# Two layers of attention and feed-forward on one core: VectorE's order inside a head of the index stage, with the selection's best-eights put between the two sums

## The reference, cut to what matters

```python
iq = (hidden_states @ idx_wq_w).reshape(b, s, IDX_H, IDX_D)          # IDX_H = 16, IDX_D = 128
ik = hidden_states @ idx_wk_w
iw = hidden_states @ idx_weights_w * IDX_H ** (-0.5)
idx_scores = jnp.einsum('bqn,bnqk->bqk', iw, jax.nn.relu(jnp.einsum('bqnd,bkd->bnqk', iq, ik))) * IDX_D ** (-0.5)
idx_scores = jnp.where(causal, idx_scores, -jnp.inf)
_, topk_idx = jax.lax.top_k(idx_scores, TOPK)                        # TOPK = 128
mask = topk_mask & causal
scores = jnp.where(mask[:, None], scores, -jnp.inf)                  # the 32 attention heads use it
```

## Time and profile before

| | us |
|---|---|
| median of three runs | 1416.42 |
| lowest and highest of them | 1415.38, 1418.27 |
| the profiled execution's own time | 1415.27 |
| its span, first to last instruction | 1413.5 |

### The profile page before, as it was taken

How to read it: one execution, slowest core, us unless ns; L and a number is a source line. 1 busy time by engine, 2 the same in 40 slices (tenths; PEclk the granted TensorE clock), 3 DMA queues, 4 the chain that set the end, 5 groups by cost and what they waited for, 6 DMA issues and landing times.

```text
span 1413.5 us, 21378 instructions
## 1 busy us (share of the span) xinstructions
PE 1308.7 (93%) x7147; PEld 1095.1 (77%) x7147; DVE 1089.0 (77%) x2246; ACT 822.2 (58%) x1816; POOL 715.1 (51%) x705
## 2 busy tenths in 40 slices
PE   4868999999899999998689999999999999999998
PEld 3756888888789887876367888888888888888876
DVE  6676334343647798999979889889899989989976
ACT  3653432222246766764567776766677676667761
POOL 3660300010037789984845665565565565566524
PEclk9978999999999999998589999999999999999999
DMA  5640300000212436646620000000000000000021
GB/s 201 208 157 27 118 13 1 1 21 0 70 39 68 125 84 198 209 141 230 207 63 14 24 6 29 29 29 29 29 13 17 29 29 29 29 29 1 16 83 60
DMA packets 83707, 95.53 MB, mean 68 GB/s; under 512 B 11792, under 2 KB 59280, under 8 KB 83088
## 3 DMA queue, kind: packets, MB, share of 16 engines
q1 hardware_dynamic: 83600, 94.17, 20.9%
HBM read 75.27 MB, written 18.87 MB: 67 GB/s over the span
## 4 chain that ended last, share of the span: by engine, by line
PE 73%; DVE 15%; ACT 3%; issue 3%; DMA 2%; POOL 1%; SPq 1%; DVEq 1%; ACTq 0%
PE ps L361 18%; PE ps L362 17%; PE ps L363 17%; PE ps L1986 9%; PE ps L2006 3%; PE ps L2005 3%; DVE rop L1523 1%; DVE xn_l L1573 1%; DVE pm L1553 1%; DVE rop L1521 1%; DVE acc L1498 1%; PE ps L1885 1%; DVE rop L1522 1%; PE ps L1684 1%; DVE top L1511 1%
## 5 line engine op out<-in xcount | busy, mean ns | idle before, releaser
L785 POOL TENSOR_SCALAR pm<-pm,smx 128x128 f32<-128x128 f32 (+1 forms) x255 | 189.3, 751 | 206.5 <-DVE smx L1560 206.4
L1114 ACT ACTIVATE pm<-pm,smx 128x128 f32<-128x128 f32 (+7 forms) x256 | 197.2, 772 | 36.6 <-DVE smx L1553 34.9
L1553 DVE CUSTOM_DVE_ANT_0 pm<-ps,mbias 128x128 f32<-128x128 f32 (+7 forms) x256 | 191.3, 752 | 27.2 <-PE ps L363 12.4
L1986 PE MATMUL ps<-ident,pm 128*128 128x128 f32 x1152 | 174.1, 276 | 7.7 <-DVE xn_l L1573 2.1
L1120 ACT ACTIVATE xn_h<-ps 128x512 fp32r<-128x512 f32 (+3 forms) x256 | 128.7, 513 | 82.1 <-PE ps L1986 79.1
L1573 DVE TENSOR_TENSOR xn_l<-ps,xn_h 128x512 fp32r<-128x512 f32 (+3 forms) x256 | 144.3, 587 | 24.3 <-ACT xn_h L1120 23.2
L1986 PEld LDWEIGHTS ps<-ident,pm 128*128 128x128 f32 x1152 | 134.0, 141 | 33.7 <-issue 11.8
L361 PE MATMUL ps<-latT_l,qc_h 128*128 128x512 f32 (+4 forms) x384 | 142.9, 372 | 16.9 <-DVE smx L1553 8.7
L363 PE MATMUL ps<-latT_h,qc_h 128*128 128x512 f32 (+4 forms) x384 | 132.4, 345 | 0.0
L362 PE MATMUL ps<-latT_h,qc_l 128*128 128x512 f32 (+4 forms) x384 | 132.2, 344 | 0.0
L361 PEld LDWEIGHTS ps<-latT_l,qc_h 128*128 128x128 f32 x384 | 73.2, 191 | 32.6 <-issue 13.1
(11 more groups left out here) (303 smaller groups left out, 3744.7 us busy)
## 6 DMA issues: line engine op xcount, KB each, us to landing
iwq_raw<-in_L_attn_idx_wq_w SPq DMA_DIRECT2D x48, 256.0 KB, 3.0
base<-in_L_ffn_mean_w SPq DMA_DIRECT2D x28, 256.0 KB, 3.4
wring<-in_L_ffn_w SPq DMA_DIRECT2D x21, 256.0 KB, 3.8
ow_raw<-in_L_attn_o_w SPq DMA_DIRECT2D x8, 512.0 KB, 3.9
xn_t<-in_L_attn_o_w SPq DMA_DIRECT2D x8, 512.0 KB, 4.2
wuvo<-pr_even SPq DMA_DIRECT2D x8, 512.0 KB, 5.0
wuvo<-pr_hl SPq DMA_DIRECT2D x8, 512.0 KB, 4.6
wuvo_h<-wuvo SPq DMA_DIRECT2D x16, 256.0 KB, 2.7
```

The costliest lines, as they stand in the source:

```text
L785: pool.tensor_scalar(pm[:, i % 4, 0:w], pm[:, i % 4, 0:w], smx[:, 32 + i:33 + i], 0.0, ALU.mult, ALU.add).then_inc(hd_p, 1)
L1114: act.activation(pm[:, i % 4, 0:w], pm[:, i % 4, 0:w], ACT.Exp, bias=smx[:, i:i + 1], scale=-1.0, accum_out=smx[:, 16 + i:17 + i]).then_in ...
L1553: dve.tensor_tensor_reduce(out=pm[:, i % 4, 0:w], in0=row_block(2 * (i % 2), t), in1=mbias[:, TRI[t]:TRI[t + 1]], scale=1.0, scalar=3.0 * BIG,
L1986: done = pe.transpose(ps[:, t_bank(p, i), tile(k)], pm[:, tq % 4, tile(4 * c + k)], ident[:])
```

## The change

In steps 16 to 47 VectorE's order in a head becomes: the sum of the first tile, all best-eights of the round, the sum of the second tile, all replacements. Before, it was both sums, all best-eights, all replacements. No instruction is added or removed, and no other engine's instructions move. At step 16 the piece of other work (`lat_work`) now stands behind the whole round.

```diff
-            def index_sum(step):
+            def index_sum(step, first, last):
                 head, tiles = step % IDXH, index_tiles(step)
-                for n, t in tiles:
+                for n, t in tiles[first:last]:
...
-            def topk_round(step):
+            def topk_max(step):
...
                     dve.max(top8[:, k, :], acc_of(t)).then_inc(tk_max, 1)
-                for k, (n, t) in enumerate(tiles):
+
+            def topk_replace(step):
+                for k, (n, t) in enumerate(index_tiles(step)):
                     dve.wait_ge(tk_max, n + 1)
...
-            for step in range(STEPS):
-                index_sum(step)
+            for step in range(IDXH):
+                index_sum(step, 0, None)
                 lat_work(step)
-                if step >= IDXH:
-                    topk_round(step - IDXH)
+            for step in range(IDXH, STEPS):
+                index_sum(step, 0, 1)
+                topk_max(step - IDXH)
+                index_sum(step, 1, 2)
+                topk_replace(step - IDXH)
+                index_sum(step, 2, None)
+                lat_work(step)
             for step in range(2 * IDXH, STEPS):
-                topk_round(step)
+                topk_max(step)
+                topk_replace(step)
```

## The result

| | before | changed |
|---|---|---|
| median of 20 runs, us | 1416.82 | 1420.87 |
| lowest and highest | 1411.96, 1418.44 | 1416.93, 1423.96 |
| profiled execution, us (span) | 1415.27 (1413.5) | 1420.45 (1418.7) |

The ratio of the times is 1.0033, 95% interval 1.0024 to 1.0043: by the ratio, the change makes the kernel slower by 4.7 us (3.4 to 6.1). The two medians lie 4.1 us apart. The forecast was +3.1.

The account below looks back on a forecast made before the run. In steps 16 to 47 VectorE and TensorE were both taken as nearly full, neither ruling alone. Terms 0.83 + 0.94 + 0.95 + 0.66 - 0.29 = 3.1 us on 1416.42 gave 1419.5 us; 8-in-10 range 1415.5 to 1424.0.

Parts of the forecast that it names:

- the three stalls: Steps 27, 36 and 41: TensorE's second-tile scores wait for VectorE's later second sum; +0.8, +0.9 and +0.9 us.
- step 27, before pair step 28: Second tile's scores held until 524.34 instead of 523.51, so step 29's first sum comes later; +0.83 us.
- step 36, before pair step 37: Second tile's matmul can start at 571.55 instead of 570.61, which VectorE cannot cover at step 38; +0.94 us.
- step 41, before pair step 42: Second tile's scores held until 599.19 instead of 598.24, the same stall as at step 36; +0.95 us.
- step 32: Second sum now stands behind tile 5's best-eight, which waits for GpSimd; +0.66 us, between 0 and 1.5.
- step 45: Wait ahead of the second sum gets filled, with ordinary steps behind it where VectorE is longer; -0.29 us.
- start of stage two and pair step 24: The filled 0.3 us wait of step 16 starts VectorE earlier, but pair step 24 takes it back; nothing.
- step 31: Its 1.10 us filled wait runs into a wait for GpSimd; its 0.8 us TensorE stall is covered; nothing.
- The cover that I had counted on: Stalls at steps 26, 30, 31, 35, 39 and 44 hidden by waits or transposes; nothing, 5.3 us if uncovered.
- No change: Rival: TensorE has more room than its busy time shows, so the three stalls vanish; +0.4 us, 1416.8, chance 0.20.
- Faster: Rival: waits ahead of the second sum go and TensorE loses nothing; -2.9 us, 1413.5, chance 0.07.
- The larger loss: Rival: none of the covered stalls is covered, each delay moves the next wait; +8.4 us, 1424.8, chance 0.13.

Follow-up runs that it names:

- No32: The changed kernel with step 32 alone back in the old order; ratio 1.0040 against the kernel before.
- no4: The changed kernel with steps 26, 32, 35 and 40 back in the old order; ratio 1.0014 against the kernel before.
- s3: The kernel before with the new order in stage three (steps 32 to 47) alone; ratio 1.0048, +6.8 us.
- rep1: The changed kernel with one replacement also moved between the two sums in steps 16 to 47; ratio 1.0087 against the kernel before, +12.3 us.
- last: The changed kernel with all replacements also ahead of the second sum in steps 16 to 47; ratio 1.0163 against the kernel before, +23.1 us.
- s2: The kernel before with the new order in stage two (steps 16 to 31) alone; ratio 1.0013, +1.8 us.

## Why the prediction was right, step by step

The sign, the mechanism and the three stalls held. The total is 3.1 us against 3.75 in the trace, since two stalls of the same kind, at steps 23 and 31, had been counted at nothing.

| term | forecast, us | in the changed kernel's trace, us |
|---|---|---|
| step 27, before pair step 28 | +0.83 | +0.82 (steps 27 to 29) |
| step 36, before pair step 37 | +0.94 | +0.95 (36 to 38) |
| step 41, before pair step 42 | +0.95 | +0.96 (41 to 43) |
| step 32 | +0.66 | +1.55 (32 to 35) |
| step 45 | -0.29 | -0.38 |
| start of stage two and pair step 24 | 0 | -0.57, then +0.82: +0.25 |
| step 31 | 0 | -0.38 |
| sum | +3.09 | +3.77 |

The middle column's three stalls come from two timelines: when the second sum would end (2.66 and 3.40 us after the first one's start) and when TensorE had wanted it (1.98 and 2.61), plus 0.15 us from the sum's end to a held matmul's start. The ends came as forecast (2.65 and 3.40). That the terms agree to 0.01 us is in part luck: the 0.15 was 0.05. Step 26's sum ends at 525.62 and the matmul starts at 525.67:

```profile
525.15 0.47 DVE L1498 SCALAR_TENSOR_TENSOR acc<-ps,iw,acc 128x256 f32<-128x256 f32 x1
```

The missing 0.1 us came back as the held matmul's longer time, 0.50 for 0.39, which the sum did not have.

*The step that was mis-sized is what stands around steps 31 and 32.* The prediction counted step 31's stall at nothing, taken up by VectorE's own 1.10 us, and step 32's moved sum at 0.66. From step 31 to step 35 the changed kernel lost 1.17 us.

The 0.66 is right as far as it goes. VectorE's wait for GpSimd ends 1.05 us late (556.27, counted from the start of step 16), because TensorE and with it GpSimd are late, and step 33's first sum is 1.71 us late, 0.66 more. The 0.38 us that the filled wait of step 31 gave is lost in that wait for GpSimd, as the prediction said, so -0.38 and a part of the +1.55 in the table cancel.

What was wrong is that VectorE's 1.10 us take up the stall of step 31. They did on VectorE, but not on TensorE, which brings 0.77 us more into step 33 and holds up VectorE at step 34 by the load. No32, with step 32 in the old order, still loses 0.70 us between steps 31 and 35, and no4 0.65. Step 32's own order is worth the other 0.47. The prediction named 1.5 us for the case that "TensorE ... lost as much again" at step 33. It lost 1.09 us there (1.89 in s3), with pair step 34 behind it, but most of that hid behind the load of step 34: the stall shows as no more than the last 0.26 us, at step 35.

*Step 24 was left out, as the statement on it was wrong.* I wrote that the pair step takes back VectorE's early start by itself. It doesn't: in the kernel with one best-eight between the sums, VectorE is 0.45 us early at step 17 and still 0.44 early at step 25. The changed kernel falls from -0.57 to +0.25, 0.82 us, the price of step 27 once more: step 23 too stands right before a pair step. That VectorE was the longer engine up to there did not protect it.

*The cover that I had counted on held* at steps 26 and 30, whose stalls (about 0.57 us each) left the next first sum where it was, at 35, and at 39 and 44, where no matmul waited. At step 31 it did not hold, as said. So TensorE's stall costs wherever an ordinary step stands right before a pair step: 23, 27, 31, 36 and 41, and 33 in s3.

*The rivals.* No change falls by the interval: weight loads are busy for 64.98 of 88.40 us in stage three now, and the room that this seems to leave did not take up waits of 0.7 us. The rule of the Trainium skill (Perfetto Trace Analysis, section Identifying the Most-Contended Engine), which goes by the weight loads, would have misled here. Faster falls; its deciding number is confirmed from both sides, since one best-eight between the sums (2.55 us forecast, 2.53 in its trace, against 2.61) costs nothing and two (3.40) do. The larger loss falls for this kernel; rep1 and last show that it comes once the delay is larger. The clock stayed at 1.00 where it mattered in the changed kernel, but the prediction's ground for that, TensorE's wait of 2.4 us in the kernel before, was no safe one: that wait stands at step 47 (629.46), and the clock fell at 635.5. In s2 it fell right behind such a wait (632.29, half from 632.9), in s3 behind one of 1.89 us, and in the changed kernel not behind 1.09. The size is right only roughly: the interval of 3.4 to 6.1 us holds the 3.75 of the trace, my 3.1 lies just below it, and whether the 0.9 us between 3.75 and the 4.7 by the ratio (0.3 to the 4.1 between the medians) arises outside these steps is open.

## What to carry to other kernels

When two engines hand buffers to each other, an instruction that frees a buffer has a due time: subtract the start of its step from the moment when the other engine used the buffer. Filling the wait ahead of it is free up to that time; past it, the price falls due wherever the other engine goes into its own long stretch next, so look at every step ahead of one, not only at those in which the first engine was seen to wait. It can reach the first engine some steps later and by a third party, here a load that is issued later. Prices of parts (here 1.8 and 6.8 us) need not add up to that of the whole (4.7): a delay of one place hides that of another, and a wait can bring TensorE's clock down in one kernel and not in the other. Compare the granted clock of each stretch before two traces are compared.

## What the runs showed of the hardware that was not expected

- TensorE's granted clock can fall inside a loop that has it at 1.00 in a kernel with the same instructions. It was 0.51 from 556.8 to 560.3 us in s3, after a wait of 1.89 us, and 1.00 in the changed kernel after 1.09 us at the same place. The 3.5 us cost TensorE about 1.6 us.
- Stretches that no edit touched differ between executions by more than the effect: the start of step 16 lies between 476.0 and 479.5 us in the thirteen profiles, and from the last best-eight to the end it took 706 to 711 us. The last rounds themselves, VectorE back to back, differ by 0.01 us (66.61 and 66.62 us from the first best-eight to the last). Differences below a few microseconds are read from one landmark to another inside the stretch, not from spans.
- One load's landing varies: ScalarE's wait for the index weights at step 30 was 0.91, 1.14 and 2.46 us in kernels that are alike up to there but for VectorE's order, and a single such wait outweighed a stall of 0.8 us.
